# Self-attention: 16 repeated rows of the heads' outputs by SyncE's transfers instead of GpSimd's copies

## What is computed

```python
Wdkv = x @ latent_w + latent_b                                  # [32, 256, 72]
q = einsum('btc,hcl->bhtl', x, Wd_w) + Wd_b[None, :, None, :]   # 16 heads of 72
scores = einsum('bhtl,bsl->bhts', q, Wdkv) / sqrt(d_head)
attn = softmax(where(causal, scores, -inf), axis=-1)
y = einsum('bhts,bsl->bhtl', attn, Wdkv)                        # a head's output, 72 rows of 256 tokens
z = transpose(y, (0, 2, 1, 3)).reshape(b, t, h * 72)
x = layernorm(x + z @ out_w + out_b)
```

## Time and profile before

| | us |
|---|---|
| median of 3 runs | 3087.67 |
| lowest and highest | 3086.12, 3088.21 |
| the profiled execution, own time | 3084.58 |
| its span, first to last instruction | 3082.8 |

### The profile page before, as it was taken

How to read it: one execution, slowest core, us unless ns; L and a number is a source line. 1 busy time by engine, 2 the same in 40 slices (tenths; PEclk the granted TensorE clock), 3 DMA queues, 4 the chain that set the end, 5 groups by cost and what they waited for, 6 DMA issues and landing times. The chain is left out here.

```text
span 3082.8 us, 72822 instructions
## 1 busy us (share of the span) xinstructions
PE 3057.7 (99%) x22529; PEld 2874.0 (93%) x22529; DVE 2255.4 (73%) x6595; ACT 2162.3 (70%) x6949; POOL 1579.3 (51%) x2918
## 2 busy tenths in 40 slices
PE   9999999999999999999999999999999999999998
PEld 7999999999999999999999999999988888889998
DVE  7888888888888777777878778788765555454665
ACT  8888888888888878888888888888844444442222
POOL 5676676666776765333333333333456666652000
PEclk9999999999999999999999999999999999999999
DMA  5455555544444461111111111111354454534333
GB/s 163 137 156 166 155 157 160 150 129 125 119 129 132 129 212 46 46 49 63 46 49 60 52 46 53 59 46 49 110 144 100 99 118 104 113 52 96 123 122 102
DMA packets 209569, 321.06 MB, mean 104 GB/s; under 512 B 36416, under 2 KB 143040, under 8 KB 208224
## 3 DMA queue, kind: packets, MB, share of 16 engines
q1 hardware_dynamic: 184672, 283.59, 30.7%
q0 software_dynamic: 24576, 33.57, 6.6%
HBM read 125.20 MB, written 75.50 MB: 65 GB/s over the span
## 5 line engine op out<-in xcount | busy, mean ns | idle before, releaser
L1214 POOL TENSOR_SCALAR ca_prob<-ca_prob,ca_inverse 128x120 f32<-128x120 f32 x1024 | 354.9, 366 | 623.9 <-DVE ca_inverse L1539 621.8
L875 ACT ACTIVATE sa_prob<-sa_prob,sa_shift 128x128 f32<-128x128 f32 (+1 forms) x1024 | 453.9, 462 | 0.0
L1480 ACT ACTIVATE ca_prob<-bank,ca_shift 128x120 f32<-128x120 f32 x1024 | 353.1, 363 | 1.7 <-DVE ca_shift L1533 0.4
L937 DVE CUSTOM_DVE_ANT_0 sa_prob<-bank,sa_mask 128x128 f32<-128x128 f32 (+1 forms) x1024 | 303.4, 351 | 5.7 <-issue 5.2
L599 POOL TENSOR_SCALAR sa_prob<-sa_prob,sa_inverse 128x128 f32<-128x128 f32 x512 | 195.2, 381 | 200.4 <-DVE sa_inverse L949 187.0
L139 PE MATMUL bank<-sa_kvT_b,sa_q 112*128 112x128 f32 (+1 forms) x1024 | 260.4, 279 | 0.0
L981 DVE TENSOR_TENSOR sa_pT_lo<-bank,sa_pT_hi 128x384 fp32r<-128x384 f32 x512 | 258.2, 544 | 0.2 <-ACT sa_pT_hi L864 0.2
L601 POOL TENSOR_SCALAR sa_prob<-sa_prob,sa_inverse 128x256 f32<-128x256 f32 x512 | 251.3, 491 | 0.0
L137 PE MATMUL bank<-sa_kvT_a,sa_q 128*128 128x128 f32 (+1 forms) x1024 | 249.4, 280 | 1.1 <-DVE sa_shift L937 0.9
L1973 POOL DMA_INDIRECT mid_acc<-ex_out,ex_to_tokens x112 | 191.0, 1705 | 89.0 <-DVE ex_out L2285 60.4
L2163 ACT ACTIVATE ex_act_g<-bank 128x512 f32<-128x512 f32 x128 | 76.5, 598 | 215.8 <-PE bank L132 205.7
(11 more groups left out here) (274 smaller groups left out, 11834.2 us busy)
## 6 DMA issues: line engine op xcount, KB each, us to landing
sa_q<-sa_q_tile SPq DMA_DIRECT2D x125, 288.0 KB
sa_q<-sa_q_tile SPq DMA_DIRECT2D x157, 112.0 KB
mid_x2T<-ca_x2T SPq DMA_DIRECT2D x32, 512.0 KB, 3.0
ex_sx<-mid_x2T SPq DMA_DIRECT2D x32, 512.0 KB, 3.4
sa_q<-sa_q_tile SPq DMA_DIRECT2D x297, 32.0 KB
sa_xT_raw<-in_xT SPq DMA_DIRECT2D x32, 256.0 KB, 3.0
sa_q<-sa_q_tile SPq DMA_DIRECT2D x32, 256.0 KB
sa_x_res<-in_x SPq DMA_DIRECT2D x32, 256.0 KB, 3.5
```

The lines of the kernel that those rows point to most:

```text
L875: act.activation(prob[:, r, hh, cols], prob[:, r, hh, cols], ACT.Exp, bias=shift[:, r, n:n + 1], scale=-1.0, accum_out=total[:, r, n:n + 1 ...
L937: dve.tensor_tensor_reduce(out=prob[:, r, hh, cols], in0=SC[hh][:, t * T:t * T + (t + 1) * P], in1=mask[:].rearrange("p a s -> p (a s)")[: ...
L1214: ins = pool.tensor_scalar(prob[:, r, t, hh], prob[:, r, t, hh], inverse[:, r, n:n + 1], 1.0, ALU.mult, ALU.mult)
L1480: act.activation(prob[:, r, t, hh], SC[g % 2][:, n * S:n * S + S], ACT.Exp, bias=shift[:, r, n:n + 1], accum_out=total[:, r, n:n + 1]).the ...
```

## The change

GpSimd's copy of 16 rows for each step goes. In its place SyncE issues one transfer for both steps of a pair (g odd), from two neighbouring places of the ring `y_hi` to two of the ring `y_lo`. It stands in slot g+10, behind the moves of that slot's query tile and ahead of the packed rows. It waits for ScalarE's copy of step g. TensorE's output products of both steps wait for its landing, and so does ScalarE before it writes a place of `y_hi` again.

```diff
+def upto_rep(J, g):
+
+    return J * (SA_BODY // 2 * 16) + 16 * (g // 2 + 1)
@@ SyncE, behind the query moves of the slot
             g = m - PL
+            if slot_exists(J, g) and g % 2 == 1:
+                y, r, own = y_at(J, g - 1), (g - 1) % RING, slice(int(packed(g) and g % QUAD == 1), 2)
+                need_alone(sp, yhi_done, upto_slot(J, g), spare_sp)
+                need(sp, o_mm, upto_slot(J, g - Y_RING))
+                sp.dma_start(f32(y_lo[AT:AT + REST, y:y + 2, own]), f32(y_hi[0:REST, r:r + 2, own])).then_inc(y_rep, 16)
             if slot_exists(J, g) and packed(g) and g % QUAD == 1:
@@ GpSimd, behind the normalising of the slot
-            g = m - PL
-            if slot_exists(J, g):
-                r = g % RING
-                need(pool, p_done, at_most(upto_slot(J, m - IL, 2), 2 * B * NP))
-                need_alone(pool, yhi_done, upto_slot(J, g), spare_pool)
-                own = slice(int(packed(g) and g % QUAD < 2), 2)
-                pool.tensor_scalar(y_lo[AT:AT + REST, y_at(J, g), own], f32(y_hi[0:REST, r, own]), 1.0, 1.0, ALU.mult, ALU.mult).then_inc(ydup_done, 1)
-                need(pool, ydup_done, upto_slot(J, g))
@@ TensorE, ahead of the output products of step g
                 need(pe, ylo_done, upto_slot(J, g))
-                need(pe, ydup_done, upto_slot(J, g))
+                need(pe, y_rep, upto_rep(J, g))
@@ ScalarE, ahead of its copy to y_hi
                 need(act, o_mm, upto_slot(J, g - RING))
+                need(act, y_rep, upto_rep(J, g - RING))
```

More of the change, by code:

```diff
@@ L359, in self_attention @@
     kv_tr, kvhi_done, kv_done = al.sem("kv_tr"), al.sem("kvhi_done"), al.sem("kv_done")
-    ydup_done = al.sem("ydup_done")
+    y_rep = al.sem("y_rep")
     y_in = al.sem("y_in")
```

## The result

The changed kernel takes 3501.14 us (median of 5, 3491.27 to 3508.35) against 3086.54 before (five runs too): ratio 1.134, 95% interval 1.132 to 1.136. The profiled execution is the longest of the five, with a span of 3506.6 us. It is 423.8 us longer than before's.

What follows compares the result with a forecast made beforehand. TensorE, never idle in self-attention, was taken as the bound. Stalls 255 + 3, end 17 and clock 45 make 320 us on the profiled 3084.6; with 3.1 us to the median, 3407.7. Range 3320 to 3530, 8 cases in 10.

Steps and rivals of the forecast that it cites:

- The clock's term: TensorE in self-attention: clock falls in the 60 stalls, 0.75 us each, 45 us in all, ends 0 and 180.
- the waits' terms: TensorE's output products waiting for the transfer: 255 us steady state, 3 us first group, 17 us end of self-attention.
- GpSimd's copies, 0: GpSimd: removing 256 copies, some 150 us of busy time off the path, gains 0, at most 2.2 us.
- The landing, 2.3 us: New SyncE transfer of 64 or 32 KB behind query moves: 2.3 us to land, ends 1.7 and 3.5.
- The four stalls of a group: TensorE waits for transfers issued in slots 3, 5, 9, 11: 4.7, 3.5, 5.6, 3.2 us, 17.0 us per 16 slots.
- The end, 17 us: End of self-attention: transfers behind cross-attention weight loads and in short slots stall TensorE 11, 4 and 2 us.
- the first group: First 16 slots of self-attention: other tile slots, with seven moves in slot 13, stall 3 us.
- the discount of three quarters: Price of a clock fall per stall taken as 0.75 us from 0 to 3, since part should meet no fall.
- the rival of stalls without the clock: Self-attention stalls occur but the granted clock stays at 1.00: 3362.7 us, chance 0.25.
- SyncE's issues: SyncE: eight query moves issued ahead of the transfer take 6.1 us, delaying it past TensorE's next output products.
- Other edits at 0: ScalarE's new wait for the transfer and SyncE's wait for ScalarE's copy cost 0; eight more issues a group fit in.
- SyncE's slack: SyncE's moves take 48 us of a group of some 72 us, leaving about 24 us.

Runs made afterwards that it cites:

- The filled waits: Changed kernel plus unread TensorE products ahead of the transfer wait: slots 4, 6, 10 and 12 filled, 3398.17 us; slots 4 and 10 alone, 3430.76 us.

## Why the prediction was right, and the term that was mis-sized

It gave 3407.7 with 3320 to 3530; measured 3501.1. Its direction, its mechanism and its places are what the runs show; the time was 93 us short. The clock's term was 115 us too small, the waits' terms 10 us too large. The time stays within the range because the clock's term had wide bounds.

- *GpSimd's copies, 0.* Right: 1.0001 without them, within 3 us.
- *The landing, 2.3 us.* Right: 2.2 us median, 2.0 to 3.0 from 100 to 1500 us. It came nearer to the small transfer's 1.7 us than to the 256 KB one's 3.1, as assumed, though the queue was not quiet: the DMA share was 0.39 to 0.51 from 964 to 968 us.
- *The four stalls of a group.* Predicted 4.7, 3.5, 5.6 and 3.2 us, measured 4.5, 3.1, 5.4 and 2.9 us, behind the slots named, and 0.4 in slot 14. That is 17.0 against 16.2 a group. Eight moves took 5.6 us where the sum had 6.1. Moving the transfer ahead of the moves, or giving it to ScalarE, left at most 0.8 us of each of the four; a second slot removed three of them and left 3.2 us of the fourth. So SyncE's order with one slot of time is shown to be the cause.
- *The end, 17 us.* Right: 11.2, 3.1 and 1.9 us in the changed kernel, and 17 us when done alone.
- *Waiting in sum.* 275 predicted, 265 measured; the first group has 6 of it, where the prediction had 3.
- *The clock, 45 us.* This is the term that was mis-sized: 160 us of slower work in the profiled execution. The wrong step was "part of the stalls should meet no fall". Of the 60 waits of the steady state in slots 4, 6, 10 and 12, 58 were followed by a fall, which came 2.1 to 4.3 us after TensorE went idle. I had the two numbers for it: the fall within 2.6 us of the last product, which all stalls exceeded, and about 6 us at the lower level at the start, which cost 3 us. Without the discount of three quarters they give 60 x 3 = 180 us, the term's upper end, and 3543 in sum, 42 us too much. The filled waits price a fall at 2.4 us, the longer busy time at 160 / 62 = 2.6. So the rival of stalls without the clock, which had 0.25, is out. The Trainium skill's "TensorE: Matmul & The Clock Gate" (section "HAM oscillation — how this bites in real kernels") was weighed too lightly. It says that a wait for a DMA between batches of products can leave the next batch at half rate. The trace agrees with it: the granted clock is 0.88 of full speed from 100 to 1500 us.
- *SyncE's issues.* Eight of them took 5.6 us in the median, two and a half times the landing of 2.2 us, and they were the mechanism. By the Trainium skill, "DMA: Bandwidth & Descriptors" (section "Issuing engines are not separate DMA queues"), a sequencer's time to initiate a DMA is usually small beside the DMA itself. For transfers of this size the trace doesn't agree: one issue of the new transfer took 0.55 us against 2.2 us to its landing, a quarter, and eight issues in a row outlast a landing.
- *Other edits at 0.* ScalarE's wait showed as 2.2 us in sum in the changed kernel, in six places. The run that adds only the issues and ScalarE's wait cost 8 us, most of it at the end, where the prediction had 0 for both. A group takes 70.8 us in the kernel before, not "some 72", so SyncE's slack was nearer to 23 us than to 24; nothing hangs on it.

## What to carry to other kernels

A transfer that replaces a copy is only as early as its place in the issuing engine's list: add up what that engine still has to issue ahead of it (0.55 to 0.8 us each here) and hold the sum against the time until the consumer, not against the transfer's bytes. One transfer for two steps saves an issue and takes the earlier step's slack away; here two small ones were 282 us cheaper. And where TensorE comes to wait for some 3 us at a time, again and again, count more than the waits: here 58 of 60 waits of 2.8 to 6.6 us were followed by a stretch at half pace, which cost 2.4 us more for each.

## What I had not expected of the hardware

Waits of only 2.9 us at the mean (slot 12) were followed by the lower level in 13 of 15 cases, and each stretch at 1.2 GHz lasted 6.1 us at the mean, though in the steady state TensorE was at work again within 4 us of its start. Over all runs, in self-attention after the first 60 us, none of 117 waits of 0.7 to 1.5 us was followed by a fall, 24 of 56 of 1.5 to 2.5 us, 59 of 74 of 2.5 to 3.3 us, and 60 of 61 longer ones (of TensorE's waits that began at the upper level; counted when the fall began during the wait or within 3 us behind it). Useless products in the waits made the kernel 103 us faster. And a transfer issued by ScalarE beside SyncE's moves took 3.1 us to land, where behind the same moves on SyncE it took 2.2.
